# First attention of a two-layer transformer block: the causal mask before the row maximum, on VectorE in place of TensorE

## The reference, cut to what matters

```
q = _unit_norm(q); k = _unit_norm(k)            # then rotary embedding on every second head
logits = einsum('bshd,bthd->bhst', q, k) * q_gain
causal = tril(ones((S, S)))
logits = where(causal, logits, finfo(float32).min)
attn = softmax(logits, axis=-1)
y = einsum('bhst,bthd->bshd', attn, v).reshape(B, S, Dm)
x = x + y @ w_out
```

## Time and profile before

| | |
|---|---|
| median of 3 runs | 1188.19 us (1181.44 to 1192.40) |
| the profiled execution | 1184.33 us, span of its trace 1182.7 us |
| first attention's scores, maxima, probabilities and output | about 119.5 to 275.2 us of the span |
| TensorE busy over the span | 77% |
| VectorE busy over the span | 61% |
| mean granted clock of TensorE | 0.89 |

### The profile page before, as it was taken

How to read it: one execution, slowest core, us unless ns; L and a number is a source line. 1 busy time by engine, 2 the same in 40 slices (tenths; PEclk the granted TensorE clock), 3 DMA queues, 4 the chain that set the end, 5 groups by cost and what they waited for, 6 DMA issues and landing times. The chain is left out here.

```text
span 1182.7 us, 23655 instructions
## 1 busy us (share of the span) xinstructions
PE 914.3 (77%) x7706; PEld 696.8 (59%) x7706; DVE 720.7 (61%) x1899; ACT 449.8 (38%) x957; POOL 489.5 (41%) x550
## 2 busy tenths in 40 slices
PE   3985899996999787896556699997989788899000
PEld 2764577765888576684445445545878676677000
DVE  5766877754888433344666689965698643345333
ACT  1553355562211344453233268881211144455000
POOL 3000422216477522332775342221577732231775
PEclk9997899997999898998677779999899998999555
DMA  6294799939964588973486467802623498985443
GB/s 238 43 172 80 152 187 220 233 130 256 214 184 142 174 259 255 284 234 119 118 202 186 76 94 114 116 7 70 153 99 107 158 265 257 266 260 175 118 131 115
DMA packets 159015, 197.06 MB, mean 167 GB/s; under 512 B 17328, under 2 KB 137648, under 8 KB 155824
## 3 DMA queue, kind: packets, MB, share of 16 engines
q1 hardware_dynamic: 99744, 94.56, 36.7%
q0 software_dynamic: 22848, 68.18, 18.2%
q10 hardware_dynamic: 36304, 32.84, 9.2%
HBM read 132.86 MB, written 90.18 MB: 189 GB/s over the span
## 5 line engine op out<-in xcount | busy, mean ns | idle before, releaser
L856 ACT ACTIVATE tmp<-ps 128x256 f32<-128x256 f32 (+1 forms) x328 | 145.5, 472 | 127.2 <-PE ps L809 37.3
L949 ACT ACTIVATE tmp<-ps 128x384 f32<-128x384 f32 (+1 forms) x256 | 135.6, 543 | 71.5 <-PE ps L622 46.9
L485 POOL DMA_INDIRECT xd<-big,slot x128 | 129.3, 1010 | 61.7 <-issue 37.8
L524 POOL DMA_INDIRECT big<-yd,slot x128 | 126.5, 988 | 42.7 <-issue 25.0
L453 POOL COPY arena<-negmax 24x2048 bf16<-24x2048 bf16 x32 | 60.5, 1892 | 175.8 <-ACT negmax L856 175.8
L603 PE MATMUL ps<-arena 96*128 96x256 bf16 (+1 forms) x512 | 106.2, 279 | 13.1 <-DVEq L290 10.6
L1086 DVE SCALAR_TENSOR_TENSOR X<-big,comb,X 128x256 f32<-128x256 f32 x128 | 59.2, 484 | 77.6 <-DMA big<-yd,slot 77.2
L1473 DVE SCALAR_TENSOR_TENSOR tmp<-tmp,ps 128x128 f32<-128x128 f32 x128 | 36.7, 287 | 113.2 <-ACT tmp L1017 112.5
L619 PE MATMUL ps<-arena 120*128 120x256 bf16 (+1 forms) x512 | 100.9, 265 | 0.9 <-POOL arena L453 0.3
L1483 DVE COPY tmp<-ps 128x256 f32<-128x256 f32 x128 | 53.6, 424 | 66.7 <-PE ps L838 36.4
L809 PE MATMUL ps<-ident,big 128*128 128x128 f32 x512 | 74.3, 290 | 25.0 <-ACT tmp L856 15.0
(11 more groups left out here) (173 smaller groups left out, 1906.5 us busy)
## 6 DMA issues: line engine op xcount, KB each, us to landing
big<-xd POOLq DMA_DIRECT2D x128, 256.0 KB, 4.9
arena<-parts SPq DMA_DIRECT2D x192, 128.0 KB, 6.0
xd<-zero SPq DMA_DIRECT2D x8, 2048.0 KB, 14.2
spill<-in_we SPq DMA_DIRECT2D x128, 128.0 KB
yd<-tmp POOLq DMA_DIRECT2D x64, 256.0 KB, 3.5
yd<-tmp ACTq DMA_DIRECT2D x64, 256.0 KB, 3.5
parts<-arena SPq DMA_DIRECT2D x128, 96.0 KB
arena<-in_we SPq DMA_DIRECT2D x8, 1024.0 KB, 8.9
```

Of the source, the lines that this page charges most:

```text
L485: pool.indirect_dma_start(xd[:, :], bass.IndirectOffsetOnAxis(ap=slot[:, i, k:k + 1], axis=0), xn_all[:, i, :], None).then_inc(scattered.s ...
L524: pool.indirect_dma_start(gring[n % GRING], None, yd[:, :], bass.IndirectOffsetOnAxis(ap=slot[:, b * TB + m % TB, m // TB:m // TB + 1], ax ...
L856: return act.activation(dst, src, ACT.Copy)
L949: act.activation(prob[h % 8][:, 0:n], ps[2 + h % 2][:, 0:n], ACT.Exp).then_inc(exp_ready.sem, 1)
```

## The change

TensorE's mask products in `scores` go. VectorE gets a tile `hide` of 256 columns, 128 zeros and then `mask_s`, and for each head, in place of one maximum over 3 x 128 columns, two operations `tensor_tensor_reduce`, one for each query block, with 128 and 256 columns. Each adds the right part of `hide` to the scores from PSUM, multiplies by -1, writes the result as bf16 into a scratch tile `masked` (which nobody reads), and gives out the minimum of the row into `mx`. So each query has one value for each head, and the merging minimum in `split_maxima` goes. A wait is added in front (the maximum before the last one, because of the scratch tile's two halves), and the building of `hide` with its wait for the constants' cast.

```
-        mx = tmp[:, 8704:8752].rearrange("p (a h) -> p a h", h=H)
+        mx = tmp[:, 8704:8736].rearrange("p (t h) -> p t h", h=H)
+        hide = sb("hide", [P, 2 * P], BF16)
+        masked = sb("masked", [P, 2, 3 * P], BF16)
...
-        both_ready = signal("both_ready")
+        hide_ready = signal("hide_ready")
...
                         mm = pe.matmul(bank[:, at:at + keys], qs[i][0:KR, h, tt * P:(tt + 1) * P],
-                                       ks[i][0:KR, h, 0:keys], start=True, stop=not causal(r))
-                        if causal(r):
-                            mm = pe.matmul(bank[:, at + keys - P:at + keys], identb, mask_s, start=False, stop=True)
+                                       ks[i][0:KR, h, 0:keys], start=True, stop=True)
                     mm.then_inc(s1_done.sem, 1)
...
                 if r == 0:
                     dve.wait_ge(later_in.sem, 16 * (len(CONSTS) - len(FIRST) - 1))
+                    dve.wait_ge(cast_done.sem, 1)
+                    dve.memset(hide[:, 0:P], 0.0).then_inc(hide_ready.sem, 1)
+                    dve.tensor_copy(hide[:, P:2 * P], mask_s).then_inc(hide_ready.sem, 1)
+                    dve.wait_ge(hide_ready.sem, 2)
...
                     if causal(r):
-                        ins = dve.tensor_reduce(mx[:, :, h], bank[:, 0:3 * P].rearrange("p (a n) -> p a n", a=3), AX.X, ALU.max, negate=True)
+                        dve.wait_ge(*mx_ready(r, b * H + h - 1))
+                        for tt in range(TB):
+                            ins = dve.tensor_tensor_reduce(masked[:, h % 2, tt * P:tt * P + tt * P + P], bank[:, tt * P:tt * P + tt * P + P],
+                                                           hide[:, P - tt * P:2 * P], -1.0, 3.0e38, ALU.add, ALU.min, mx[:, tt, h:h + 1])
...
                     dve.wait_ge(*mx_ready(r, b * H + 8 * q + 8))
-                    if causal(r):
-                        low = mx[:, 1, 8 * q:8 * q + 8]
-                        dve.tensor_tensor(low, low, mx[:, 2, 8 * q:8 * q + 8], ALU.min).then_inc(both_ready.sem, 1)
-                        dve.wait_ge(both_ready.sem, n + 1)
```

## The result

The changed kernel takes 1176.32 us (median of 13 runs, 1168.31 to 1187.27) against 1187.47 us for the kernel before (13 runs, 1178.29 to 1196.47): a ratio of 0.992, 95% interval 0.989 to 0.995. It is faster by 0.8%. Some executions run slower than the rest; the ratios leave them out (one of 13 on each side here), the medians do not. The number forecast was 1185; 1176 is where rival A ended (1177), and just inside the lower end of the range, 1176.

What follows compares the result with a forecast made beforehand. TensorE bounds the first attention now, VectorE after the change. About six steady batches give -5 us and batch 0 adds 1.9, so -3 us: 1185 us from the median 1188.19, range 1176 to 1206.

Steps and rivals of the forecast that it cites:

- rival A: First attention: the row minimum comes free, 0.55 us a head on VectorE, TensorE stays the bound; 1177 us, chance 0.10.
- What bounds: First attention's steady batches: TensorE sets the pace at 17.65 us; after the change VectorE becomes the bound at 16.8 us.
- What is removed: TensorE's two mask products per head ahead of the maximum: 1.86 us a batch, leaving 15.8 us for TensorE.
- The slot: VectorE's time for one head's two masked minima: 0.55 us streaming plus 2 x 0.075 for the row minima, 0.70 us.
- The bounds: Limits on VectorE's time for a head: 0.55 us if the row minimum is free, up to 1.03 us.
- The two-engine sum: A steady batch: VectorE's 5.2 us plus 16 x 0.70 plus 0.4 for waits on TensorE, 16.8 us, against TensorE's 15.8.
- break-even: VectorE's time for a head at which the steady batches gain nothing, staying at 17.65 us: 0.75 us.
- Batch 0: First attention's first batch: VectorE alone sets the pace, the first eight maxima get 1.9 us later, the second eight cost nothing.
- The stall: VectorE's wait in batch 0 for GpSimd's cast, 3.42 us for an operation of 0.17; forecast about 1.4 us.
- Small edits: Building the hiding tile and the added waits: hidden in VectorE's idle time, nothing, or 0.3 us once without that cover.
- The clock (C): Rival: TensorE waits more and drops to 1.2 GHz, losing 2 us in each of seven batches; 1199 us, chance 0.05.
- The stage as the kernel's change: What follows the first attention starts after a barrier, so that stage's change, -3 us, is the whole kernel's.

Runs made afterwards that it cites:

- Kernel 1: The kernel before with TensorE's mask products ahead of the maximum removed and nothing in their place: 1289.91 us against 1297.67 before, ratio 0.998.
- kernels 3 and 4: The changed kernel with one more unread VectorE copy from PSUM per head, 72 or 216 columns: 1298.21 and 1312.78 us against 1297.67 before, ratios 1.003 and 1.014.
- Kernel 7: The changed kernel with GpSimd's cast of marks between batch 0's second split and the copy of that half's maxima: 1267.50 us, 0.985 of the kernel before.
- the repeat: The changed kernel measured once more beside the kernel before: 1177.53 us against 1185.94, ratio 0.994.
- kernel 8: The changed kernel with GpSimd multiplying odd heads' probabilities by 0 or 1 in place of TensorE's mask products: 1281.14 us, 0.993 of the kernel before.
- kernel 5: The changed kernel with GpSimd's cast of marks moved behind the copy of batch 0's second half of maxima: 1175.67 us, 0.992 of the kernel before.
- kernel 6: The changed kernel with GpSimd multiplying all heads' probabilities by 0 or 1 in place of TensorE's mask products: 1193.17 us, 1.008 of the kernel before.

## Why the prediction was right in its range and wrong in the step

The measured 1176.32 us lies 0.3 us inside the range, whose lower end was set by rival A and not by the forecast. The forecast itself, 3 us down, missed the 11 us that were gained, and that the range still held is luck: its mechanism for the steady part, VectorE as the next bound, was wrong.

**What bounds.** Right: TensorE, before and after. The forecast that VectorE would take over was wrong.

**What is removed.** Two products at 0.058 us for each head were to give 1.86 us a batch. TensorE's busy time fell by 1.79 (17.54 to 15.75) and the period by 1.67, as its idle time grew from 0.11 to 0.23 us. Kernel 1 gives the same 15.98 without the addition, so the missing 0.2 us are TensorE's own and no coupling to the new operations.

**The slot: the step that failed.** The row minimum's small step ("I take 0.075 us") put the slot, VectorE's time for a head, at 0.70; it measured 0.556. The small step exists and is 83 ns long, slightly more than taken, but occupies nothing: it starts together with the next main operation. The bounds held, at their lower end; the error was to choose by duration a step whose price is its spacing, after having said for the products that spacing counts. By the Trainium skill, VectorE: DVE Perf Modes, section "Two Vector instructions with no wait between them", an operation that writes its accumulator is two instructions, which the trace shows; I read from it that the lower end falls away, and it does not. The same section says when an instruction has to wait for the ones in front, namely when it starts in another quadrant (of 32 partitions) than the last access to the same memory; here all start at partition 0, and in the rows the main operations are not held (285 ns long, followed after 0.21 us), which agrees. The prediction's other doubt, that one instruction of a head becomes four, came to little: 0.556 us against 0.464.

**The two-engine sum.** Right, by kernels 3 and 4: 17.02 for 16.8, 18.77 for 19.0, break-even at 0.75 (that -2.9 us met -3 is partly luck, as said there). At 0.556 VectorE needs 5.2 + 8.9 = 14.1 us by that sum (13.5 busy in the trace), below TensorE's 15.98. That is rival A: 12 less 0.7 forecast, 10.9 measured in the stage, which is its 6.5 batches at the 1.67 us that a batch really gained. It had a chance of 0.10, too low: its lower end was not an extreme case but what happens when nothing holds the small step.

**Batch 0.** "VectorE alone sets the pace already" was wrong for the first eight maxima. They took 4.22 us up to the next operation (120.47 to 124.69), the second eight 3.83 (125.61 to 129.44), and in kernel 1, without the mask products, the first eight 3.84: TensorE set their pace, at 1.2 GHz and 0.53 us for a head's products (its L603 products of 128 columns start at 120.65, 121.19 and 121.72), against VectorE's 0.464. With the change they take 4.57 us (121.60 to 126.17), 0.35 more, not 1.9. The stall was to fall to 1.4 us as the maxima in front of it got longer; they did so by less, and it fell from 3.42 to 2.81 only. From the stage's start to the end of the held operation it is 14.58 us before (118.28 to 132.86) and 14.84 after, and to the end of the split 15.43 and 15.46: batch 0 costs nothing, where the sum had 1.9 us. Kernel 7 shows what the stall was worth: 3 us.

**Small edits.** The copy that builds the hiding tile took 0.43 us in place of 0.20, beside GpSimd's memsets. The first maximum started 2.01 us after the stage's start, against 2.19 before: it is hidden, as said.

**The clock (C).** From the stage's start to the end of the stall TensorE's granted clock was 0.50 (1.2 GHz), against 0.80 before in the same part; batch 0 took no longer, so it cost little there. From the stall to 157.5 us it was 0.87 on average, against 0.93 before in the same part (132.86 to 157.92); as an estimate from these two, 0.13 x 23.1 less 0.07 x 25.1, the change lost some 1.2 us more to the lower clock there, once. In the batches shown it was 1.00. The loss in each batch did not come.

**The stage as the kernel's change.** The medians say so: -11.2 us against -10.9 in the stage; the ratio gives -9.4, with an interval from -6 to -13 us, and the repeat -7.5. So the total is compatible with the stage, but it does not prove that nothing is given back. The profiled execution gained 2.75 us only, since its combination stage was 8.5 us longer; this shows how little one execution's total says.

## What to carry to other kernels

An operation whose result falls out of an accumulator costs the engine its streaming time, as long as nothing waits for it at once: price it by the spacing of its neighbours and keep the duration for whoever waits. Moving work off a full engine gains until the next engine's sum passes it, and that sum, slot by slot, is good to a few per cent; but it must be made for the engine that gives the slack (GpSimd at 0.73 us for each head had none), for what its operations hold up on a neighbour (VectorE's split, 0.65 us for 0.17), and, as kernel 8 suggests, for the chain too. When the period of the main loop is settled, look at the start: one cast of another engine, moved behind the operation that it holds up, brought 3 us in each attention.

## What the runs showed of the hardware

- The accumulator's read on VectorE: 83 ns long (256 of them), no slot of its own. The masked minimum of 128 and of 256 columns from PSUM is followed after 0.21 and 0.345 us, the same as an addition of that size.
- GpSimd's cast of 24 x 4096 elements (3.60 us) holds a VectorE cast of 16 columns from SBUF to SBUF until it ends (2.81 us for 0.17; 2.11 in kernel 5), while the masked minima, with one input from PSUM and one from SBUF, run beside it at full speed. The Trainium skill, SBUF — State Buffer, section "Who interferes with whom", says that a VectorE operation with at most one SBUF input, outside the modes with two ports, does not contend with GpSimd, and that casts can enter these modes; the rows agree. The merging L1230, with two SBUF operands, was held in the same way. GpSimd's multiplication (two SBUF operands) holds the split's operations too, 0.65 us for 0.17, but not the masked minima (0.28 and 0.42 us in kernel 6).
- GpSimd's multiplication of 128 x 256 f32 elements took 0.73 us, VectorE's addition of that size 0.42.
- The kernel before took about 1187 us here and 1290 to 1298 on two other chips. The first attention had no part in that: the change's period here and that of kernel 7 there are the same 15.98 us, and the waits without a counterpart in the traces here are ScalarE's (releaser remote). What they are was not settled.
